# Second attention of a fused two-block layer kernel: fp32 scores in row groups, probabilities normalised on GpSimd, V stationary in four column groups, and a batch loop written out

## The reference, cut to what matters

```python
kv_d = x @ kv_d_w                       # 512 -> 128
q_d = x @ q_d_w
k_p = (kv_d @ k_u_w).reshape(b, s, NH, RD)      # NH = 16 heads, RD = 16
q_p = (q_d @ q_u_w).reshape(b, s, NH, RD)
v = (kv_d @ v_u_w).reshape(b, s, NH, HD)        # HD = 32
k_r = apply_rope((x @ rope_k_w).reshape(b, s, NH, RD), cos, sin)
q_r = apply_rope((q_d @ rope_q_w).reshape(b, s, NH, RD), cos, sin)
k = concatenate([k_p, k_r]); q = concatenate([q_p, q_r])
scores = einsum('bqhd,bkhd->bhqk', q, k) * scale     # causal mask
out = einsum('bhqk,bkhd->bqhd', softmax(scores), v).reshape(b, s, H)
return out @ o_w
```

## Time and profile before

| what | us |
|---|---|
| median of three runs | 2123.91 |
| profiled execution | 2125.45 |
| its span | 2123.7 |
| PE busy in the span | 1885.2 |
| DVE busy | 1377.2 |
| ACT busy | 994.7 |
| POOL busy | 786.7 |

### The profile page before, as it was taken

One profiled execution on the slowest core, in us unless ns is written; L12 is line 12 of the kernel. 1 busy time (PEld: TensorE's weight loads), 2 busy tenths in 40 slices (PEclk: granted clock), 3 DMA queues, 4 the chain that ended last, 5 costly groups with the idle time before them and its releaser, 6 DMA issues. The chain is left out here.

```text
span 2123.7 us, 27520 instructions
## 1 busy us (share of the span) xinstructions
PE 1885.2 (89%) x9226; PEld 1238.9 (58%) x9226; DVE 1377.2 (65%) x2196; ACT 994.7 (47%) x1736; POOL 786.7 (37%) x1057
## 2 busy tenths in 40 slices
PE   7878665998999899997999899898899999899895
PEld 3446443695458565695447555496446666588442
DVE  5766698574563799574664699577554499667411
ACT  1412774462322786363232698264142399355021
POOL 1146377441210276561120177372020157472201
PEclk9989755998999999998999999999899999899898
DMA  6337100000213185200213176210022257310683
GB/s 259 109 115 245 52 0 20 1 2 1 99 45 119 57 266 173 96 25 22 79 51 119 35 244 227 84 41 21 17 97 93 69 175 263 127 41 21 237 311 104
DMA packets 55072, 221.09 MB, mean 104 GB/s; under 512 B 6288, under 2 KB 6288, under 8 KB 46992
## 3 DMA queue, kind: packets, MB, share of 16 engines
q1 hardware_dynamic: 45776, 195.14, 26.5%
q0 software_dynamic: 5120, 16.78, 2.4%
q10 hardware_dynamic: 4032, 7.34, 0.9%
HBM read 179.65 MB, written 39.58 MB: 103 GB/s over the span
## 5 line engine op out<-in xcount | busy, mean ns | idle before, releaser
L1933 POOL TENSOR_TENSOR Y<-Y,HC 128x1024 f32<-128x1024 f32 x116 | 273.9, 2362 | 174.0 <-DVE HC L1336 173.4
L1325 DVE TENSOR_TENSOR_SCAN HS<-DA,ps 128x1024 f32<-128x1024 f32 x128 | 292.3, 2284 | 23.5 <-PE ps L742 13.0
L534 PE MATMUL ps<-ring,XNT 128*128 128x512 f32 x384 | 182.4, 633 | 21.0 <-issue 12.2
L1688 ACT ACTIVATE DA<-DL,AB,AN 128x511 f32<-128x511 f32 x256 | 193.8, 806 | 14.8 <-DVE HS L1325 13.5
L954 PE MATMUL ps<-ring,XBT 128*128 128x512 f32 x384 | 188.5, 597 | 0.0
L1801 ACT ACTIVATE PD<-ps,NMX 128x128 f32<-128x128 f32 (+3 forms) x256 | 135.1, 530 | 101.2 <-DVE NMX L1470 99.2
L1470 DVE TENSOR_REDUCE NMX<-ps 128x1 f32<-128x128 f32 (+3 forms) x256 | 124.3, 487 | 65.4 <-PE ps L805 65.1
L823 PE MATMUL ps<-V,PTD 128*128 128x33 f32 x1280 | 164.2, 262 | 0.0
L823 PEld LDWEIGHTS ps<-V,PTD 128*128 128x128 f32 x1280 | 162.6, 192 | 0.5 <-ACT PTD L839 0.5
L650 PE MATMUL ps<-XNH,tern 128*128 128x512 f32 x352 | 139.2, 396 | 9.8 <-DVE tern L1225 5.4
L534 PEld LDWEIGHTS ps<-ring,XNT 128*128 128x128 f32 x384 | 76.6, 204 | 117.4 <-issue 108.1
(11 more groups left out here) (248 smaller groups left out, 4026.0 us busy)
## 6 DMA issues: line engine op xcount, KB each, us to landing
ring<-experts_dram SPq DMA_DIRECT2D x48, 1024.0 KB, 5.1
tern<-tern_q SPq DMA_DIRECT2D x33, 768.0 KB, 4.2
ring<-experts_dram SPq DMA_DIRECT2D x48, 512.0 KB, 5.4
RAW<-tern_dram SPq DMA_DIRECT2D x22, 768.0 KB, 4.8
ring<-wqkv_dram SPq DMA_DIRECT2D x4, 3072.0 KB, 11.9
XB<-xg SPq DMA_DIRECT2D x42, 256.0 KB, 3.6
yg<-YB SPq DMA_DIRECT2D x42, 256.0 KB, 4.9
tern_q<-tern SPq DMA_DIRECT2D x11, 768.0 KB, 7.0
```

Source lines behind the costliest of these rows:

```text
L534: last = pe.matmul(ps[:, 2 + 3 * (i % 2) + part], XNT[:, k, tile(i)], wqkv[:, k, part * C:(part + 1) * C], start=(k == 0), stop=(k == NK - 1))
L1325: v.tensor_tensor_scan(HS[:, q].rearrange("p j t -> p (j t)"), DA[:, q].rearrange("p j t -> p (j t)"), ps[:, 2 * q:2 * q + 2].rearrange("p ...
L1688: s.activation(DA[:, u % 2, jj, 1:T], DL[:, j, 1:T], ACT.Exp, scale=AN[:, j * NS + n:j * NS + n + 1], bias=AB[:, j * NS + n:j * NS + n + 1 ...
L1933: p.tensor_tensor(y, y, HC[:, q], ALU.add).then_inc(c_y, 1)
```

## The change

D is built anew, in `pe_D`, `v_D`, `s_D` and `p_D`:

- Q and K are turned as they are (fp32, 4 heads of 32 rows per 128) into `QT` and `KT`. The high and low stacks and their casts on POOL are gone.
- The heads go in 8 pairs (`heads_of(p)`), as in stage A. A pair has three units, `D_TILES`: query tile 3; tiles 2 and 0; tile 1. So there are 24 units (`NU`), each for both heads `x` = 0, 1. Their fp32 scores come from row groups of 32 (`pe_D_scores`) in banks 2 to 7.
- DVE takes the maxima of both heads in one instruction (`v_D_max`). ACT's exponential also sums each row into `DEN` (`s_D_exp`), DVE inverts it (`v_D_recip`), and POOL multiplies the probabilities in place (`p_D_scale`).
- Three units later (`DEPTH`) PE turns them (`pe_D_turn`), head 0 in bank 0 and head 1 in bank 1; DVE copies head 0, ACT head 1 (`copy_p`) into `PTD`.
- After two pairs PE multiplies for four heads with V stationary, 32 columns per head in four column groups (`pe_D_pv`), the probabilities moving, into bank 7. The result is already transposed; ACT copies it to `AOTD`. The heads' transposes are gone.
- The projection of the first three groups of four heads stands before the last units' turns (`pe_D_project`); only the last quarter is left for the end (`pe_project_D`). DVE's base for the sum (`ACC`) stands inside the loop. The gathers of expert rows are issued before the first unit.
- The batch loop is written out: `for b in range(1, B)` in place of `nc.Fori(1, B)`.

The core of the diff (the functions that only leave are not shown):

```diff
+D_TILES = ((3,), (2, 0), (1,))
+NU = len(D_TILES) * NP
+DEPTH = 3
+NEXT_AT = {14 + 2 * i: i for i in range(NT)}
+def d_parts(k):
+    p, m = divmod(k, len(D_TILES))
+    for i in D_TILES[m]:
+        n = (i + 1) * P
+        col = 3 * P if i == 0 else 0
+        yield i, n, [(x, 2 + 2 * m + x, col) for x in range(2)]
...
+    T_BANK[_key] = _key[2] if _key[0] == "p" else _n % 2
...
+            for k in range(NU + DEPTH + 1):
+                if k < NU:
+                    pe_D_scores(pe, k)
+                if k >= 9 and k % 6 == 3:
+                    pe_D_pv(pe, k // 6 - 1)
+                if DEPTH <= k < NU + DEPTH:
+                    pe_D_turn(pe, k - DEPTH)
+                if k in NEXT_AT:
+                    pe_norm(pe, 0, NEXT_AT[k])
+                if k in (NU, NU + 1):
+                    pe_D_project(pe, (0, 1) if k == NU else (2, 3))
...
+        def pe_D_scores(pe, k):
+            p = k // len(D_TILES)
+            if k >= len(D_TILES):
+                pe.wait_ge(d_exp, k - len(D_TILES) + 1)
+            if k >= 11 and k % 6 == 5:
+                pe.wait_ge(d_head, k // 6)
+            for i, n, places in d_parts(k):
+                for (h, rows), (_, bank, col) in zip(heads_of(p), places):
+                    pe.matmul(ps[:, bank, col:col + n], QT[rows, h // 4, tile(i)], KT[rows, h // 4, 0:n],
+                              start=True, stop=False, skip_group_check=True)
+                for _, bank, col in places:
+                    last = pe.matmul(ps[:, bank, col + n - P:col + n], identb, mask_q, start=False, stop=True,
+                                     skip_group_check=True)
+            last.then_inc(d_scores, 1)
+        def pe_D_turn(pe, k):
+            pe.wait_ge(d_scaled, k + 1)
+            for x in range(2):
+                bank = t_bank(pe, ("p", k, x))
...
+                        last = pe.transpose(ps[:, bank, place:place + P], probs(places[x])[:, tile(kt)], ident)
+                last.then_inc(t_full, 1)
+        def pe_D_pv(pe, g):
+            for x in range(2):
+                t_emptied(pe, ("p", 6 * g + 5, x))
+            pe.wait_ge(d_exp, min(6 * g + 9, NU))
+            if g:
+                pe.wait_ge(d_head, g)
+            for kt in range(NT):
+                n = (NT - kt) * P
+                for r in range(4):
+                    first = 16 - 4 * kt if r // 2 else 5 * kt
+                    last = pe.matmul(ps[32 * r:32 * r + 32, 7, kt * P:T], VD[:, kt, (4 * g + r) * HD:(4 * g + r + 1) * HD],
+                                     PTD[:, r % 2].rearrange("p s q -> p (s q)")[:, first * P:first * P + n],
+                                     start=(kt == 0), stop=(kt == NT - 1), skip_group_check=True)
+            last.then_inc(d_pv, 1)
+        def pe_D_project(pe, tiles):
+            pe.wait_ge(d_head, NK - 1)
+            pe.wait_ge(d_exp, NU - 2 if tiles[0] == 0 else NU - 1)
+            for i in tiles:
+                for k in range(NK - 1):
+                    pe.matmul(ps[:, 2 + i], AOTD[:, k, tile(i)], wo1[:, k], start=(k == 0), stop=False,
+                              skip_group_check=True)
...
+            for k in range(NU + DEPTH):
+                if k < NU:
+                    v_D_max(v, k)
+                if 1 <= k <= NU:
+                    v_D_recip(v, k - 1)
+                if k >= DEPTH:
+                    copy_p(v, v.tensor_copy, k - DEPTH, 0)
+                if experts and 3 <= k < 3 + 2 * NT:
+                    v_combine(v, k - 3)
...
+            for k in range(NU + DEPTH + 2):
+                if k < NU:
+                    s_D_exp(s, k)
+                if DEPTH <= k < NU + DEPTH:
+                    copy_p(s, s.copy, k - DEPTH, 1)
...
+                if k >= 10 and k % 6 == 4:
+                    g = k // 6 - 1
+                    s.wait_ge(d_pv, g + 1)
+                    s.copy(AOTD[:, g], ps[:, 7]).then_inc(d_head, 1)
...
+        def s_D_exp(s, k):
+            s.wait_ge(d_max, k + 1)
+            p = k // len(D_TILES)
+            if k >= DEPTH:
+                s.wait_ge(t_full, T_INDEX["p", k - DEPTH, 1] + 1)
+            for i, n, places in d_parts(k):
+                for x, bank, col in places:
+                    c = d_column(i, x)
+                    ins = s.activation(probs(places[x])[:, 0:n], ps[:, bank, col:col + n], ACT.Exp,
+                                       bias=NMX[:, p % 2, c:c + 1], accum_out=DEN[:, p % 2, c:c + 1])
+            ins.then_inc(d_exp, 1)
+        def p_D_scale(p, k):
+            p.wait_ge(recip_done, k + 1)
...
+                ins = p.tensor_tensor(both, both, RDN[:, pair % 2, c:c + 2].rearrange("p (x o) -> p x o", o=1)
+                                      .to_broadcast([P, 2, n]), ALU.mult)
+            ins.then_inc(d_scaled, 1)
...
-        with nc.Fori(1, B) as b:
-            step(x_rows[bass.ds(b + 1, 1)].rearrange("o p i c -> (o p) i c"),
-                 out_rows[bass.ds(b - 1, 1)].rearrange("o p i c -> (o p) i c"), True)
+        for b in range(1, B):
+            step(x_rows[b + 1], out_rows[b - 1], True)
```

More of the change, by code:

```diff
@@ L113 @@
           + list(d_transposes())
-          + [(("heads", 1, i), "act") for i in range(NT)]
           + [(("norm", 4, i), "act") for i in range(NT)])
@@ L181, in build @@
     RN = small("RN", [P, NT, 32])
[L182 to L183 removed]
+    NMX = small("NMX", [P, 2, 8])
+    DEN = small("DEN", [P, 2, 8])
+    RDN = small("RDN", [P, 2, 8])
     AN = small("AN", [P, NK * NS])
@@ L489, in pe_norm @@
             last.then_inc(t_full, 1)
-        def pe_stack(pe, g, i):
-            pe.wait_ge(stack_ready, 2 * (NT * g + i + 1))
-            bank = t_bank(pe, ("stack", 1, g, i))
-            for j in range(2 * GH):
-                last = pe.transpose(ps[:, bank, tile(j)],
-                                    STK[:, i, j].rearrange("p a d -> p (a d)").bitcast(F32),
-                                    ident)
-            last.then_inc(t_full, 1)
         def pe_project_A(pe):
@@ L830, in pe_D, with pe_D_qk @@
                 pe_norm(pe, 4, i)
-        def copy_p(eng, copy, v):
-            key = ("p", v)
-            eng.wait_ge(t_full, T_INDEX[key] + 1)
-            if v >= 3:
-                eng.wait_ge(d_pv, v - 2)
-            n = (v % NT + 1) * P
-            copy(PTD[:, v % 3, 0:n], ps[:, T_BANK[key], 0:n]).then_inc(t_free[T_ENGINE[key]], 1)
+        def pe_D_qk(pe, i):
+            pe.wait_ge(qn_ready, NT + i + 1)
+            pe.wait_ge(p_copied, i + 1)
+            for z in range(2):
+                bank = t_bank(pe, ("qkd", i, z))
+                for g in range(NK):
+                    h = NH * z + 4 * g
+                    last = pe.transpose(ps[:, bank, tile(g)], QN[:, i, h:h + 4].rearrange("p h d -> p (h d)"), ident)
+                last.then_inc(t_full, 1)
@@ new lines, in pe_D_turn @@
+        def pe_D_turn(pe, k):
[3 more added lines that the diff above has]
+                for i, n, places in d_parts(k):
+                    at = 3 * P if i == 0 else 0
+                    for kt in range(i + 1):
+                        place = at + (i - kt if x else kt) * P
+                        last = pe.transpose(ps[:, bank, place:place + P], probs(places[x])[:, tile(kt)], ident)
+                last.then_inc(t_full, 1)
@@ new lines, in copy_p @@
+        def copy_p(eng, copy, k, x):
+            key = ("p", k, x)
+            p = k // len(D_TILES)
+            eng.wait_ge(t_full, T_INDEX[key] + 1)
+            if p >= 2:
+                eng.wait_ge(d_pv, p // 2)
+            for i, n, places in d_parts(k):
+                at = 3 * P if i == 0 else 0
+                first, step = (16 - 4 * i, 5) if x else (i, 4)
+                ins = copy(PTD[:, p % 2, first:first + step * i + 1:step],
+                           ps[:, T_BANK[key], at:at + n].rearrange("p (m q) -> p m q", q=P))
+            ins.then_inc(t_free[T_ENGINE[key]], 1)
@@ L1507, in v_D, with v_D_max, v_D_recip @@
                     v_normalize(v, 4, i - 1)
+        def v_D_max(v, k):
+            v.wait_ge(d_scores, k + 1)
+            p, m = divmod(k, len(D_TILES))
+            for i, n, places in d_parts(k):
+                _, bank, col = places[0]
+                c = d_column(i, 0)
+                ins = v.tensor_reduce(NMX[:, p % 2, c:c + 2], ps[:, bank:bank + 2, col:col + n], AX.X, ALU.max, negate=True)
+            ins.then_inc(d_max, 1)
+        def v_D_recip(v, k):
+            v.wait_ge(d_exp, k + 1)
+            p, m = divmod(k, len(D_TILES))
+            c = d_column(D_TILES[m][0], 0)
+            n = 2 * len(D_TILES[m])
+            v.reciprocal(RDN[:, p % 2, c:c + n], DEN[:, p % 2, c:c + n]).then_inc(recip_done, 1)
         def v_route(v):
```

257 lines of the change are left out of this document (74 added, 183 removed).

## The result

The changed kernel takes 2244.3 us (median of 4 runs, 2242.9 to 2245.4) where the kernel before takes 2123.2 in the same session: ratio 1.0575, 95% interval 1.0555 to 1.0595. It is 121 us slower; 2113 was predicted, so the forecast missed by 131 us and in sign.

A forecast was written before the change was run, and what follows sets the result against it. An ACT-PE chain was to bound D's loop: 93.5 us against 86.1, +7.4 a step; tail -8.2; written-out loop -7.5 once. From 2125.45 that gives 2114.8, less 1.5 for the median 2113 us; 8-in-10 range 2072 to 2150.

The forecast's parts named there:

- PE's work: In D's loop: PE busy about 70 of some 93 us; 6.9 a pair of heads against 10.2 before.
- The rival of pairs: Product with V: four column groups go only in pairs, 4.6 us a product, kernel 2148, slower; chance 18%.
- Row sums: ACT's exponentials: 0.1 us each, 0.8 a pair; rival of a separate read-out: 0.13 more each, 2146, chance 15%.
- POOL and DVE off the path: In D's loop: both lie beside the chain; POOL's scaling 6.3 us a pair, 51 in all, under the loop's 93.
- The chain: D's loop: exponential, copy, turn, next exponential follow one another, 7.9 us a pair; rival that it is hidden: 2035, 15%.
- About 0.5 until the next scores in bank 7 are through: At three products with V in D's loop: the last part of 3.8 us each, 11.4 together.
- the order copy behind exponential: On ACT: the copy of unit k-4 stands behind the exponential of unit k-1, a link of the chain.
- the buffer that I put at its centre: Probabilities: unit k's exponential waits until PE has turned unit k-3, because it overwrites the same buffer.
- The clock: PE in D's loop: upper clock, 1.00 before; a fall to 1.2 GHz would make the prediction wrong; no chance given.
- Tail: Behind D's loop: 16.0 us where 24.2 stood, -8.2 a step.
- Loop over batches: Barriers between steps: writing the loop out saves 7.5 us once; rival that the barrier stays as long: 2121, chance 10%.
- the forecast had put 0: Before D's loop: Q and K turns, 3.6 us of PE instead of 1.8, mostly in waits for the rope; net 0.

The follow-up runs named there:

- e5: Changed kernel with ACT's copy of a turned unit ahead of the next exponential and the product with V copied out at once; 2149.2 us, ratio 1.0105.
- e12: e5 with DVE's expert sums spread, next norm a unit later, product with V behind the turns, its copy behind the next exponential; 2147.6 us, ratio 1.0121.
- e4: Changed kernel with a second buffer for the probabilities, so exponentials wait for turns 6 units back instead of 3; 2232.6 us, ratio 1.0497.
- e10: Changed kernel with each score matmul on all 128 rows, so the heads' scores no longer run side by side; 2204.2 us, ratio 1.0353.
- e9: Changed kernel with both heads' scores on the first head's 32 rows, so they no longer run side by side; 2365.3 us, ratio 1.1133.
- e3: Changed kernel with useless 128-row matmuls on PE before scores, turns and the waits for bank 7; 2206.2 us, ratio 1.0387.
- e6: e5 with 3 useless matmuls a unit, 1 before the scores and 2 before the turns; 2149.2 us, ratio 1.0094.
- e14: e12 with DVE's expert sum ahead of the reciprocal, plus useless full matmuls before scores and turns; 2119.2 us, ratio 0.9977.

## Where the prediction was right and where it was wrong

- **PE's work.** Right: 71 us a loop at the upper clock against 70. Four column groups do run together: the last product with V of the first loop, at the upper clock, is

```profile
524.03 2.36 PE L835 MATMUL ps<-PTD,VD 128*32 128x512 f32 x32 [0.51 <-DVE PTD L865]
```

2.36 us for four heads, forecast 2.4. The rival of pairs (4.6) falls, and so does the estimate of 2.7 from the Trainium skill (TensorE: Matmul & The Clock Gate, Part 3): the trace is a little better than it.
- **Row sums.** The term was right and the picture half wrong. They are read out by an instruction of their own, but two exponentials of 512 columns with it start 0.68 apart:

```profile
438.55 0.69 ACT L1842 ACTIVATE PD<-ps,NMX 128x512 f32<-128x512 f32 x1 [6.36 <-PE ps L821]
439.13 0.19 ACT L1842 ACTIVATION_READ_ACCUMULATOR PD<-ps,NMX 128x1 f32 x1
439.23 0.68 ACT L1842 ACTIVATE PD<-ps,NMX 128x512 f32<-128x512 f32 x1
```

The read-out begins 0.11 before the exponential ends and costs 0.1, as booked.
- **POOL and DVE off the path.** Right for the changed kernel: its 1024-column scaling takes 1.89 us, less than the 2.36 of the earlier trace rows; the first loop, without expert sums, is as long as the others. In the faster loops DVE is no longer beside the path: most of PE's waits are for its copies of turned tiles (8.5 of 11.7 us in e5's second loop, 9.5 of 13.2 in e12's).
- **The chain.** Its members were right: ACT waits 200 of 233 us before exponentials for PE's turns. Two of its terms were too small. "About 0.5 until the next scores in bank 7 are through" was a wait of 3.4 us twice and 1.3 once in each loop, since ACT takes that copy up behind two exponentials. And the order copy behind exponential, which I took as given, was worth more than the buffer that I put at its centre (e5 69 us, e4 12), the former mostly through the clock.
- **The clock.** This is the step that failed. The prediction carried the clock of the earlier trace rows, 1.00 at 3% idle, into a loop for which it forecast 25% idle, and made its fall a condition of being wrong, without a price or a chance. It would have cost one line: 70 us of PE work at 1.2 GHz is 140, so a loop bound by PE at a clock of 0.5 to 0.7 takes 100 to 140. What the runs showed in its place is a clock of 0.68 in the loop: 71 us of work took 105.5, and the loop 123.9 instead of 93.5. The idle share is not enough to explain it: with the scores on 128 rows PE was idle longer (e10, 23.2 us a loop) at a clock of 0.90, with all of them on the rows of one head it was idle 15.2 us at 0.62 (e9). It is the 32-row matmuls in a loop with waits; by what measure the chip weighs them is not shown. Nothing in the rows ahead of the prediction showed that; stage A has the same pairs at the full clock. Once the clock is low, every turn takes nearly twice as long (1.91 us for eight instead of 1.10), and ACT waits for the turns.
- **Tail.** Right: four tails take 62.6 us against 94.4 before, 8.0 a step (8.2 booked).
- **Loop over batches.** Right in the traces of both kernels, right within the error in the times of the changed one, not there in the times of the kernel before.

The books, for the profiled executions: of the 131 us, 122 are the loops', 1 the tails', and some 9 lie ahead of the loops: from a step's first matmul to D's first scores there are 1522 us in all against 1512. Of these 9, 6 are in D itself: from its first matmul to its first scores each step takes 1.5 us more (30.12 against 28.64 in the second), where the forecast had put 0. The other 3 are open; the rest cancels to within 2 us.

## What to carry to other kernels

Before work is taken off an engine that was busy without a gap, ask what it will wait for afterwards, and price the work that is left at PE's lower clock as well as at its upper: if that is more than the chain, the lower clock is a rival that needs a chance of its own, above all where the matmuls use few rows. On an in-order engine, put the instruction whose input is ready ahead of the one whose input is still being made; here that one swap was worth 3% of the kernel. When the clock column of a loop is below 1 though PE is almost always busy, a few useless matmuls on all rows are a cheap test of what the clock costs; they gave 38 us in e3, nothing in e6 and 33 in e14.
